# A sparse attention kernel: direct rows weighted and added on ScalarE and VectorE, half of the lists made inside layer 0, gathers of layer 1 bounded to four tiles ahead, roots for four tiles at once

## What is computed

```python
def _gnn_ref(neuron_states, adjacency, Wq, Wk, Wv):
    q = neuron_states @ Wq.T
    k = neuron_states @ Wk.T
    v = neuron_states @ Wv.T
    mask = adjacency.T
    scores = jnp.where(mask, q @ k.T, NEG)
    attn = jax.nn.softmax(scores, axis=1)
    attn = jnp.where(mask, attn, 0.0)
    return attn @ v

x = _layernorm(x + _gnn_ref(x, adj, L0_gnn_Wq, L0_gnn_Wk, L0_gnn_Wv), axis=-1)
x = _layernorm(x + _gnn_ref(x, adj, L1_gnn_Wq, L1_gnn_Wk, L1_gnn_Wv), axis=-1)
```

## Time and profile before

| | |
|---|---|
| median of three runs | 357.2 us (353.58 to 357.67) |
| the profiled execution | 355.52 us |
| its span in the profile | 353.8 us |
| busy in the span | PE 210.2, PEld 178.2, DVE 142.0, ACT 97.5, POOL 99.4 us |
| granted clock of TensorE, mean | 0.777 of full speed |

### The profile page before, as it was taken

One profiled execution on the slowest core, in us unless ns is written; L12 is line 12 of the kernel. 1 busy time (PEld: TensorE's weight loads), 2 busy tenths in 40 slices (PEclk: granted clock), 3 DMA queues, 4 the chain that ended last, 5 costly groups with the idle time before them and its releaser, 6 DMA issues.

```text
span 353.8 us, 4213 instructions
## 1 busy us (share of the span) xinstructions
PE 210.2 (59%) x1302; PEld 178.2 (50%) x1302; DVE 142.0 (40%) x813; ACT 97.5 (28%) x281; POOL 99.4 (28%) x114
## 2 busy tenths in 40 slices
PE   2856798234297797888985553000009888878670
PEld 2644577134187686776863343000008777776660
DVE  0138329530436644576434132000003666439423
ACT  1202035040133434544434120000003344344322
POOL 3547004777360000000000577777720000000000
PEclk9978579755569899999998758555555999887885
DMA  8997101333130000000000233333310000000001
GB/s 241 305 322 233 30 0 42 95 104 104 39 97 0 8 25 30 30 14 19 30 31 31 89 105 95 98 104 103 99 50 0 2 31 31 30 30 10 22 31 63
DMA packets 20953, 24.95 MB, mean 71 GB/s; under 512 B 1984, under 2 KB 17856, under 8 KB 20928
## 3 DMA queue, kind: packets, MB, share of 16 engines
q0 software_dynamic: 4608, 12.59, 12.8%
q1 hardware_dynamic: 16320, 12.06, 11.5%
HBM read 20.45 MB, written 4.19 MB: 70 GB/s over the span
## 4 chain that ended last, share of the span: by engine, by line
PE 45%; another core or an unknown queue 19%; ACT 11%; DVE 11%; issue 9%; DMA 3%; POOL 0%; POOLq 0%; ACTq 0%; DVEq 0%
PE PS L956 15%; PE PS L967 9%; PE PS L850 8%; PE PS L920 3%; ACT weight L392 3%; ACT y_sb L410 3%; PE PS L829 2%; DVE near L724 2%; PE PS L841 2%; PE PS L941 2%; DMA adj_words<-in_adj 2%; ACT weight L402 2%; ACT Q L338 1%; ACT exps L382 1%
## 5 line engine op out<-in xcount | busy, mean ns | idle before, releaser
L967 PE MATMUL PS<-WvT,y_sb 128*128 128x256 f32 x128 | 33.7, 408 | 57.2 <-ACT y_sb L410 57.2
L694 DVE SCALAR_TENSOR_TENSOR X<-PS,inv,X 128x256 f32<-128x256 f32 x32 | 15.4, 480 | 113.6 <-PE PS L967 113.3
L281 POOL DMA_INDIRECT xd<-x_rows,d_row x32 | 32.0, 1001 | 102.0 <-DMA x_rows<-X 92.6
L956 PE MATMUL PS<-weight,xd 128*128 128x128 f32 x256 | 47.9, 318 | 14.5 <-ACT weight L402 14.5
L967 PEld LDWEIGHTS PS<-WvT,y_sb 128*128 128x128 f32 x128 | 24.1, 198 | 63.3 <-ACT y_sb L410 60.4
L956 PEld LDWEIGHTS PS<-weight,xd 128*128 128x128 f32 x256 | 41.5, 231 | 20.1 <-issue 20.1
L850 PE MATMUL PS<-M,xt 128*128 128x256 f32 x128 | 38.2, 451 | 2.2 <-ACT xt L331 1.4
L281 POOL DMA_INDIRECT xd<-in_x,d_row x32 | 32.1, 1005 | 21.2 <-DVE d_row L516 12.1
L410 ACT ACTIVATE y_sb<-PS 128x512 f32<-128x512 f32 x16 | 9.6, 597 | 92.3 <-remote 52.3
L644 DVE CUSTOM_DVE_ANT_0 prod<-Q,xd,d_none 128x256 f32<-128x256 f32 x64 | 29.8, 475 | 12.9 <-DMA xd<-x_rows,d_row 12.9
L850 PEld LDWEIGHTS PS<-M,xt 128*128 128x128 f32 x128 | 28.1, 228 | 7.8 <-ACT xt L331 1.8
(11 more groups left out here) (124 smaller groups left out, 302.7 us busy)
## 6 DMA issues: line engine op xcount, KB each, us to landing
adj_words<-in_adj SPq DMA_DIRECT2D x4, 1024.0 KB, 8.1
X<-in_x SPq DMA_DIRECT2D x2, 1024.0 KB, 7.6
x_rows<-X SPq DMA_DIRECT2D x8, 256.0 KB, 2.1
out<-X SPq DMA_DIRECT2D x8, 256.0 KB, 2.1
W<-in_L_gnn_Wq SPq DMA_DIRECT2D x2, 256.0 KB, 5.9
W<-in_L_gnn_Wk SPq DMA_DIRECT2D x2, 256.0 KB, 5.0
xd<-in_x,d_row POOLq DMA_INDIRECT x32
W<-in_L_gnn_Wv SPq DMA_DIRECT2D x2, 256.0 KB
```

The costliest lines, as they stand in the source:

```text
L281: pool.indirect_dma_start(xd[:, t, k, :], None, rows, bass.IndirectOffsetOnAxis(ap=d_row[:, t, k:k + 1], axis=0), bounds_check=N - 1, oob_ ...
L694: dve.scalar_tensor_tensor(out=X[layer + 1][:, t, :], in0=PS[:, 5, j * D:j * D + D], scalar=inv[:, t:t + 1], in1=X[layer][:, t, :], op0=AL ...
L956: last = nc.tensor.matmul(PS[:, 4, at_h:at_h + P], rows, weight[:, n % 2, j, k, :], start=(k == 0), stop=(k == S))
L967: last = nc.tensor.matmul(PS[:, 5, j * D:j * D + D], y_sb[:, n % 2, j, h, :], WvT[:, layer, h, :], start=(h == 0), stop=(h == H - 1))
```

## The change

- SP loads the second quarter of `adj` ahead of the weights and of `x`. The last pair of a layer is stored on a semaphore of its own, `normed_last`.
- POOL, layer 0: the direct gathers of half 0, its overflow, the direct gathers of half 1, its overflow, as before, now written out; `bounds_check` is gone from all gathers. Layer 1: from the fifth tile on POOL waits for the DVE products of the tile four back (AHEAD = 4).
- DVE's first part (the top words of `overflow_codes`) is a function of its own, `more_words`. Ahead of layer 0 stand only the lists of half 0 and `more_words(1)`. The rest of half 1 goes into layer 0: `overflow_codes(1)` behind pair 0, its offsets, starts, distances and ownership in stage 1, its list products and `what_edges_get(1)` in stage 2, `own_t` in stages 2 and 3.
- Queries: pairs 0 to 3 ahead of layer 0, pairs 4 to 7 in its stages 0 to 3; those of layer 1 for pairs 0 to 3 in stages 6 to 9 of layer 0, for pairs 4 to 7 in stages 0 to 3 of layer 1. Layer 1's products of the weights move to stages 4 and 5.
- `scatter` puts only the overflow scores through PE (two matmuls); DVE adds the mask of empty slots to them (`slot_scores`) and `tops` reads the slots in SBUF.
- `direct_weights` is gone. ACT multiplies the first direct row by its exponential (`first_rows`), DVE adds the second one times its own (`both`), and `sums` runs eight matmuls in place of twelve: the one row through the identity, the overflow row through its weights.
- The norm chain runs once for four tiles, in twelve levels spread over two stages; for the last pair DVE runs it in one piece and does the last step too (`last_norm`). PE's `expand` of the next pair stands ahead of `tops_of_edges`.

The core of the diff:

```diff
             adjacency(0)
+            adjacency(1)
...
                 pool.indirect_dma_start(xo[:, t, :], None, rows,
-                                        bass.IndirectOffsetOnAxis(ap=e_row[:, t:t + 1], axis=0),
-                                        bounds_check=N - 1, oob_is_err=False).then_inc(o_in[t], 16)
-
-            for h in range(HALVES):
-                for c in (2 * h, 2 * h + 1):
-                    pool.wait_ge(s["directs"], c + 1)
-                    for t in range(QT * c, QT * c + QT):
-                        direct(x, t)
-                pool.wait_ge(s["listed"], h + 1)
-                for t in range(HT * h, HT * h + HT):
-                    overflow(x, t)
+                                        bass.IndirectOffsetOnAxis(ap=e_row[:, t:t + 1], axis=0)).then_inc(o_in[t], 16)
+
+            for c in (0, 1):
+                pool.wait_ge(s["directs"], c + 1)
+                for t in range(QT * c, QT * c + QT):
+                    direct(x, t)
+            pool.wait_ge(s["listed"], 1)
+            for t in range(HT):
+                overflow(x, t)
+            for c in (2, 3):
+                pool.wait_ge(s["directs"], c + 1)
+                for t in range(QT * c, QT * c + QT):
+                    direct(x, t)
+            pool.wait_ge(s["listed"], 2)
+            for t in range(HT, T):
+                overflow(x, t)
 
             pool.wait_ge(s["x1_stored"], 16 * PAIRS)
             for t in range(T):
+
+                if t >= AHEAD:
+                    pool.wait_ge(s["s_done"], (S + 1) * (T + t - AHEAD + 1))
                 direct(x1_dram, t)
                 overflow(x1_dram, t)
...
+            def first_rows(layer, p):
 
                 n = layer * PAIRS + p
                 act.wait_ge(s["totalled"], 2 * (n + 1))
-                need(act, "y_ready", 2 * (n - 1))
-                for j in range(2):
-                    for k in range(S):
-                        act.activation(weight[:, n % 2, j, k, :], ident[:, :], ACT.Copy,
-                                       scale=exps[:, n % 2, j, k:k + 1]).then_inc(s["a_ready"], 1)
+                for j in range(2):
+                    act.activation(first_row[:, n % 2, j, :], xd[:, 2 * p + j, 0, :], ACT.Copy,
+                                   scale=exps[:, n % 2, j, 0:1]).then_inc(s["first_in"], 1)
...
             direct_rows(0)
             direct_rows(1)
+            more_words(0)
             overflow_codes(0)
             direct_rows(2)
             starts(0)
             direct_rows(3)
             ownership(0)
+            more_words(1)
             what_edges_get(0)
-            overflow_codes(1)
-            starts(1)
-            ownership(1)
-            what_edges_get(1)
...
+            def slot_scores(layer, p):
+
+                n = layer * PAIRS + p
+                dve.wait_ge(s["sk_ready"], n + 1)
+                dve.tensor_tensor(slots[:, n % 2, :, S:SLOTS], PS[:, 2, 0:2 * KO].rearrange("p (j k) -> p j k", j=2),
+                                  no_slot[:, 2 * p:2 * p + 2, :], ALU.add).then_inc(s["masked"], 1)
...
+            def both(layer, p, j):
+
+                n = layer * PAIRS + p
+                if j == 0:
+                    need(dve, "y_ready", 2 * (n - 1))
+                dve.wait_ge(s["first_in"], 2 * n + j + 1)
+                dve.scalar_tensor_tensor(out=both_rows[:, n % 2, j, :], in0=xd[:, 2 * p + j, 1, :], scalar=exps[:, n % 2, j, 1:2],
+                                         in1=first_row[:, n % 2, j, :], op0=ALU.mult, op1=ALU.add).then_inc(s["both_in"], 1)
...
-                elif level in (4, 6, 8):
+                elif level in (3, 6, 9):
+                    c = chain(dve.tensor_tensor(square[:, :], guess[:, now, :], guess[:, now, :], ALU.mult))
+                elif level in (4, 7, 10):
+                    c = chain(dve.tensor_tensor(near[:, :], square[:, :], less_half[:, :], ALU.mult))
+                elif level in (5, 8, 11):
...
+                        norm_part(layer, p, i)
+                    edge_scores(layer, p)
+                    if layer == 0 and p == 1:
+                        starts(1)
+                    if layer == 0 and p == 2:
+                        what_edges_get(1)
                     if among(p - 1):
                         residual(layer, p - 1, 0)
-                    norm_level(layer, p - 2, 7)
-                    if among(p):
-                        tops(layer, p)
-                    norm_level(layer, p - 2, 8)
+                    slot_scores(layer, p)
+                    tops(layer, p)
                     if among(p - 1):
                         residual(layer, p - 1, 1)
-                    norm_level(layer, p - 2, 9)
-                    if among(p):
-                        below_top(layer, p)
+                    below_top(layer, p)
                     if among(p - 1):
                         row_stats(layer, p - 1, 0)
+                    inverses(layer, p)
+                    both(layer, p, 0)
+                    both(layer, p, 1)
+                    if among(p - 1):
                         row_stats(layer, p - 1, 1)
-                    if among(p):
-                        inverses(layer, p)
-                    if layer == 0 and p == PAIRS:
+                    if layer == 0 and p == 0:
+                        overflow_codes(1)
+                    if layer == 0 and p == 1:
+                        ownership(1)
+                    if layer == 0 and p == 5:
                         capacity()
...
             pack_part(0)
+            pack_part(1)
             pe.wait_ge(s["w_first"], 32)
             product(0, 4)
             pe.wait_ge(s["x_in"], 16)
+            transposes(0)
+            transposes(1)
             pe.wait_ge(s["m_sb"], 1)
-            transposes(X0, 0)
-            transposes(X0, 1)
             queries(0)
-            pack_part(1)
-            transposes(X0, 2)
+            transposes(2)
             queries(1)
-            transposes(X0, 3)
+            pack_part(2)
+            transposes(3)
             queries(2)
-            pack_part(2)
+            pack_part(3)
+            offsets(0)
             queries(3)
-            pack_part(3)
-            pe.wait_ge(s["x_rest_in"], 16)
-            transposes(X0, 4)
-            transposes(X0, 5)
-            queries(4)
-            offsets(0)
-            transposes(X0, 6)
-            queries(5)
             lists(0)
-            transposes(X0, 7)
-            queries(6)
-            queries(7)
+            pe.wait_ge(s["keyed"], 1)
+            own_turns(0)
+            own_turns(1)
             pe.wait_ge(s["w_in"], 64)
-            pe.wait_ge(s["q_sb"], PAIRS)
-            turned(0, 6)
-            product(1, 7)
-            offsets(1)
-            pe.wait_ge(s["m_sb"], 2)
-            turned(1, 6)
-            lists(1)
+            turned(0, 5)
...
+                need(pe, "masked", n)
+                for j in range(2):
+                    last = nc.tensor.matmul(PS[:, 2, j * KO:(j + 1) * KO], own_t[:, 2 * p + j, :], score_k[:, n % 2, j, :],
+                                            start=True, stop=True)
                 last.then_inc(s["sk_ready"], 1)
...
-                    pe.wait_ge(s["a_ready"], 6 * n + 5 + j)
+                    pe.wait_ge(s["both_in"], 2 * n + j + 1)
+                    pe.wait_ge(s["a_ready"], 2 * n + j + 1)
                     for h in range(H):
                         at_h = j * D + h * P
-                        for k in range(S + 1):
-                            rows = xd[:, t, k, h * P:h * P + P] if k < S else xo[:, t, h * P:h * P + P]
-                            last = nc.tensor.matmul(PS[:, 4, at_h:at_h + P], rows, weight[:, n % 2, j, k, :],
-                                                    start=(k == 0), stop=(k == S))
+                        nc.tensor.matmul(PS[:, 4, at_h:at_h + P], both_rows[:, n % 2, j, h * P:h * P + P], ident[:, :],
+                                         start=True, stop=False)
+                        last = nc.tensor.matmul(PS[:, 4, at_h:at_h + P], xo[:, t, h * P:h * P + P], weight[:, n % 2, j, :],
+                                                start=False, stop=True)
...
+        def turned_for(layer, p):
+
+            if layer == 0:
+                return QUADS + p if p < QUADS else PAIRS + p - 6 if 6 <= p < 10 else None
+            return PAIRS + QUADS + p if p < QUADS else None
...
-                        pe.wait_ge(s["normed"], 2 * (p - 3) + 2)
-                        transposes(X1, PAIRS + p - 3)
+                for p in range(PAIRS + 2):
+                    z = turned_for(layer, p)
                     if among(p - 1):
                         projected(layer, p - 1)
+                    if layer == 0 and p == 0:
+                        pe.wait_ge(s["x_rest_in"], 16)
+                    if layer == 0 and p == 1:
+                        offsets(1)
+                    if layer == 0 and p == 2:
+                        lists(1)
```

(13 more changed lines are left out.)

299 lines of the change are left out of this document (170 added, 129 removed).

## The result

The kernel after took 314.46 us (312.05 to 314.99 in four runs) against 356.8 for the kernel before, a ratio of 0.8815 with an interval of 0.8742 to 0.8888. The forecast was 303, range 270 to 332. The profiled execution took 314.92 us, its span is 313.2, 40.6 less than the span of before.

A forecast was written before the change was run, and what follows sets the result against it. The prediction took holes in PE's work during runs of POOL's gathers to bound the kernel. From 355.5 us, terms of -38, +23, -4, -33, +4 and -3 gave 304.5; less 1.5 for unspent allowances, 303 us, range 270 to 332.

The forecast's parts named there:

- What bounds: Whole kernel: holes in PE's work, not busy shares, set the time; PE's completions seem held while gathers follow closely.
- -33 for the hole: Layer 1, first gather to second neg_top: POOL's limit of four tiles shortens 73.8 us to 41, -33 (-45 to -20).
- +4 for the later pairs: Layer 1, second to eighth neg_top: gathers now run beside pairs 2 to 5, 66.7 us against 62.9, +4 (-8 to +35).
- The first pair: Start to first neg_top: layer 0 waits only for half 0's lists, from 99.25 to 61, -38 us (-42 to -34).
- Layer 0: First to eighth neg_top: takes over half 1's lists (87 us) plus a hold of 10; 98 against 75.3, +23 (+8 to +30).
- A pair: Interval between neg_tops without a query: 16 passes instead of 24 in the sums; 9.3 us becomes 8.4 (7.9 to 9.5).
- The ends: Layer 0's eighth neg_top to layer 1's first gather, 22.2 to 18.5 us, -4; last neg_top to the end, -3.
- The 1.5 us that I took off: On the sum of 304.5 us: three terms carry wide positive allowances that won't all be spent, so 1.5 us less.
- A: Rival, both layers: breaks in the gathers are enough and PE is never held; 267 us, chance 0.22.
- B: Rival, layer 1: the limit does nothing, the cause lies elsewhere, for instance code loading; hole stays 50 us; 333 us, chance 0.10.
- C: Rival, layer 1: limit and hold lock into each other, a period of about 20 us a pair; 363 us, chance 0.07.
- D: Rival, both layers: the new DVE work decides, 10.5 us a pair; 330 us, chance 0.11.

The follow-up runs named there:

- chip B: Follow-up chip without holds: the kernel before takes 276.0 us; the kernel after without POOL's limit of four tiles in layer 1 takes 246.0 us.
- four variants: The kernel after without the limit 246.0 us, with AHEAD = 2 245.9, with layer 0's second half paced 247.0, with all layer 0 gathers paced 246.4.
- chip C: Follow-up chip with holds: the kernel before takes 351.2 us, the kernel after unchanged 310.6, the kernel after without POOL's limit in layer 1 332.9.
- plain loads: The kernel after with layer 1's 48 gathers replaced by SP loads of the same size, rows in order: 280.1 us where before takes 355.2.

## Why the prediction was right, and where it wasn't

**What bounds.** Right, and shown: what lies under and behind the runs of gathers, not the busy shares, set the time on this chip. Only the second hole stands at 0 in the earlier trace rows, though; in the first PE's digits are 2 to 4, so it was slowed rather than stopped. And that completions are held was argued, not shown: already the packing of the earlier trace rows was slow without one between its matmuls. The limit is worth 22 us on after (333 against 311). I had -33 for the hole and +4 for the later pairs, 29 in sum. The terms of after itself came out at -33.5 and +5.3; it is the kernel without the limit that does better than before did (73.8 and 62.9), its second neg_top 71.3 us after the first gather and the later pairs at 57.6 in sum, with no gathers beside them. The working of -33 came out step by step: the first run took 30.3 us (31 forecast), y_sb came 34.2 us after the first gather (36) and the second neg_top 6.2 later (5).

**The first pair: -38 forecast, -35.4 measured.** Half 0's rows came at 56.6 (55 forecast). What I didn't see is that this stretch too is full of holds: on a chip without them the first neg_top stands at 47.0. Under the first 16 gathers of after DVE's top words wait 11.1 us for `remote`, and M reaches ACT at 22.7 where without holds it is there at 16.1. I read the slow packing of the earlier trace rows as a small effect and took it as it stood. That -38 came out so close has to do with it: before was held there too (99.25 against 72.6 on chip B).

**Layer 0: +23 forecast, +28.7 measured.** This is the step that went wrong, and that the sum came near is luck: its two errors, -12 and +19, nearly cancel. Without holds the seven intervals take 75.2 us (46.99 to 122.15 on chip B, the same code in layer 0), where I had 87: the codes and lists of half 1 hide better in the pairs than priced. And the hold isn't 10 us but 104.1 - 75.2 = 28.9, 19.8 of it in the first interval (33.5 against 13.7). I let one run cost something once; the trace shows `remote` waits of 8.7, 14.9 and, under the eight gathers of half 1's overflow, 6.7 us on ACT in layer 0, and half the clock behind them. The eight passes of the first projection behind the hold and of one far from any:

```profile
91.35 3.78 PE L1044 MATMUL PS<-WvT,y_sb 128*128 128x256 f32 x8 [11.92 <-ACT y_sb L430]
```

```profile
244.19 1.99 PE L1044 MATMUL PS<-WvT,y_sb 128*128 128x256 f32 x8 [0.69 <-ACT y_sb L430]
```

The same work takes 3.78 us at 1.2 GHz, where PE had stood idle for 12 us, and 1.99 at 2.4 GHz. A hole is paid for twice.

**A pair: 8.4 forecast, 7.9 measured** without a query (the earlier trace rows had 9.3), 9.9 with one. Both 9.3 and 7.9 are the shortest intervals of their kernels and not typical ones: the last six of layer 1 average 10.5 us in before, and after's last three are 8.3, 9.4 and 10.8. The direct rows gave 1.2 of the 1.4, where I had 1.0 for the passes and 0.25 against it for the mask. The query's 2.1 came out as 2.0.

**The ends.** -3.6 and -2.1 where I had -4 and -3. The 1.5 us that I took off for allowances not spent had no ground; no run shows the term, and in sum the allowances were overspent. Together with +2.6, +5.7 and +1.3 on the terms above this makes most of the 12 us by which 303 was too low.

**The rivals.** A (PE is never held) is false here and true on the two chips where before takes 275. After itself wasn't run there, but its four variants that differ in the pace of the gathers alone took 0.89 to 0.91 of before (the one without the limit by its median, 246.0 of 276.0), mostly by the earlier start (72.6 to 47.0). Whether after itself is as fast there stays open. B (the limit does nothing) fell on chip C, where the limit gives 22 us. Its example, code loading, finds no support: around the end of the three holes (258 to 266 in before, 216 to 221 in after, 240 to 248 without the limit on chip C) no instruction queue moved a packet. C: the new waits of POOL come to 32.7 us, and one interval of layer 1 is 19.3 us (247.24 to 266.57), under a run of 12 gathers that two waits released one behind the other; behind the first the others are 8 to 11, so nothing locks for good, but one period of C's kind did occur. D: the two rows cost DVE 480 ns each, and PE waited for them 3.0 us in all.

## What to carry to other kernels

Look at what ends a `remote` wait before reading busy shares: here the longest, 52.3 and 40.6 us, ended 5 us behind a run of POOL's gathers, and the shorter ones within some 4 us behind one or in its middle, whoever waited. Where a chip shows this, don't issue gathers earlier than they are needed. Four waits that spread layer 0's took 15 us off, and a break after every six in layer 1 took the ratio from 0.947 to 0.840; where holds are absent the variants lay within 1.1 us of each other. And look at a change on more than one chip before crediting one part of it: on chip C the limit is worth 22 of some 40 us, and on chip B a ratio as good comes without it.

## What the runs showed of the hardware that I had not expected

One program takes 351 to 357 us on some chips and 274 to 276 on others, with the same gathers at nearly the same pace (1.25 us each without `bounds_check`, 98 and 109 GB/s). For one program traced on both kinds, the difference of 88.8 us lies in the stretches with runs of gathers alone. Waits there last up to 52.3 us. It isn't only late news of PE's work: sixteen DVE instructions without a wait among them started over 10.5 us in place of 1.2, and PE's packing matmuls were slowed as well. Why some chips do this wasn't found, nor by what path. The runs exclude the number of bytes (264 GB/s of plain loads hold nothing) and the program's own waits as the whole cause (one kernel, both pictures), and show that runs of six with a break of 2.7 us leave no `remote` wait over 3.05 us in layer 1. The rule of the Trainium skill that the prediction weighed, "SBUF — State Buffer", section "Who interferes with whom", that DMA doesn't contend with a compute engine, agrees with the plain loads. Its rule that PE never waits on anyone, which stands in a section on SBUF's ports, doesn't describe the chips with holds, where PE's work, or the news of its end, waits for POOL's gathers; whether a port has anything to do with it, no run here shows.
